# The expert table's layout and its fetch, and new setup lists, in a one-core transformer block

## The reference, cut to what matters

```python
# x: (32, 512, 256), float32; D = 256, F = 512, E = 8 experts
h = layernorm(x) * (1 + ca) + sa                      # per row, modulation from c @ wmod
S = scan(s = a*s + (1-a)*h)                            # over the 512 tokens
x = x + ga * (S @ W.T + b + conv5(h) + conv_b)
h = layernorm(x) * (1 + cb) + sb
sel = argmax(gelu(h[:, -1] @ Wp1 + bp1) @ Wp2 + bp2)   # one expert of 8 for each row
y = gelu(h @ W1[sel] + b1[sel]) @ W2[sel] + b2[sel]
x = x + gb * (h + 0.3 * (y @ Wo + bo))
```

## Time and profile before

| | us |
|---|---|
| median of 3 runs (lowest, highest) | 654.22 (653.48, 655.22) |
| the profiled execution, its own time | 653.61 |
| its span, first to last instruction | 651.8 |
| TensorE, busy in the span | 633.2 |
| VectorE / ScalarE / GpSimd, busy | 568.0 / 551.1 / 439.4 |

### The profile page before, as it was taken

How to read it: one execution, slowest core, us unless ns; L and a number is a source line. 1 busy time by engine, 2 the same in 40 slices (tenths; PEclk the granted TensorE clock), 3 DMA queues, 4 the chain that set the end, 5 groups by cost and what they waited for, 6 DMA issues and landing times.

```text
span 651.8 us, 11098 instructions
## 1 busy us (share of the span) xinstructions
PE 633.2 (97%) x3405; PEld 521.6 (80%) x3405; DVE 568.0 (87%) x895; ACT 551.1 (85%) x976; POOL 439.4 (67%) x536
## 2 busy tenths in 40 slices
PE   7898899999999999999999999999999999999996
PEld 7686687888788888888888888888888888888865
DVE  1686889999899999999999999999999999998712
ACT  3797788889888988889988988888988898887763
POOL 2774676776677676776667667677666767677543
PEclk9999999999999999999999999999999999999999
DMA  9999635455445455455544545554544455543442
GB/s 297 329 358 298 212 135 194 139 186 167 166 158 191 162 193 194 148 185 175 172 165 163 189 167 194 176 185 158 194 146 170 171 175 183 193 162 111 172 165 104
DMA packets 55454, 120.58 MB, mean 185 GB/s; under 512 B 5643, under 2 KB 43364, under 8 KB 46180
## 3 DMA queue, kind: packets, MB, share of 16 engines
q1 hardware_dynamic: 51844, 115.65, 51.9%
q10 hardware_dynamic: 3552, 4.23, 2.0%
HBM read 61.12 MB, written 25.19 MB: 132 GB/s over the span
## 4 chain that ended last, share of the span: by engine, by line
PE 84%; DMA 7%; POOL 3%; DVE 2%; ACT 2%; issue 1%; SPq 1%; DVEq 0%; ACTq 0%; POOLq 0%
PE U L1062 10%; PE U L1063 9%; PE U L1064 9%; PE Q L1077 9%; PE Q L1078 8%; PE Q L1082 8%; PE TR L1102 8%; PE Q L1094 4%; PE Y L1046 4%; PE Y L1043 4%; PE Y L1042 4%; PE TR L1094 4%; DMA up_w<-up_table 3%; DMA xr<-in_L_attn_x_dram 2%; DMA xr<-in_L_ffn_W_dram 2%; PE U L1117 2%
## 5 line engine op out<-in xcount | busy, mean ns | idle before, releaser
L452 POOL TENSOR_TENSOR g_lo<-g,g_hi 128x512 fp32r<-128x512 f32 x128 | 173.8, 1358 | 90.0 <-ACT g_hi L613 85.0
L839 DVE SCALAR_TENSOR_TENSOR Y<-h,taps,Y 128x512 f32<-128x512 f32 x320 | 224.7, 750 | 2.9 <-PE Y L1046 0.7
L1062 PE MATMUL U<-hid_hi,up_w 128*128 128x512 f32 x256 | 107.4, 419 | 2.2 <-DMA up_w<-up_table 2.2
L1077 PE MATMUL Q<-g_hi,down_w 128*128 128x512 f32 x256 | 106.2, 415 | 0.0
L565 ACT ACTIVATE S<-xr,nmr,rstd 128x256 f32<-128x256 f32 x128 | 66.6, 592 | 42.6 <-POOL S_lo L460 40.1
L1063 PE MATMUL U<-hid_hi,up_w 128*128 128x512 f32 x256 | 101.4, 396 | 0.0
L1078 PE MATMUL Q<-g_hi,down_w 128*128 128x512 f32 x256 | 101.1, 395 | 0.0
L1064 PE MATMUL U<-hid_lo,up_w 128*128 128x512 f32 x256 | 100.8, 394 | 0.0
L787 DVE BATCH_NORM_STATS2 st<-xr 128x6 f32<-128x512 f32 x128 | 88.4, 712 | 9.4 <-DMA xr<-in_L_attn_x_dram 4.9
L606 ACT ACTIVATE g<-U,up_w 128x512 f32<-128x512 f32 x128 | 88.1, 688 | 8.6 <-PE U L1064 7.0
L435 POOL TENSOR_SCALAR rstd<-st 128x4 f32<-128x4 f32 x64 | 26.5, 413 | 87.2 <-DVE st L787 84.5
(11 more groups left out here) (115 smaller groups left out, 1293.7 us busy)
## 6 DMA issues: line engine op xcount, KB each, us to landing
up_w<-up_table SPq DMA_DIRECT2D x32, 1027.0 KB, 6.2
down_w<-down_tab SPq DMA_DIRECT2D x32, 1024.0 KB, 4.7
xr<-in_L_attn_x_dram SPq DMA_DIRECT2D x32, 512.0 KB, 3.6
out_dram<-xr SPq DMA_DIRECT2D x64, 256.0 KB, 2.3
xr<-in_L_ffn_W_dram ACTq DMA_DIRECT2D x5, 512.0 KB, 11.6
xr<-in_L_ffn_W_dram SPq DMA_DIRECT2D x4, 512.0 KB, 9.4
up_table<-g_lo SPq DMA_DIRECT2D x2, 1024.0 KB, 10.2
up_table<-down_w SPq DMA_DIRECT2D x2, 1024.0 KB, 9.3
```

The lines of the kernel that those rows point to most:

```text
L452: nc.gpsimd.tensor_tensor(g_lo[:, f], g[:, f % 2], g_hi[:, f].bitcast(f32), ALU.subtract).then_inc(g_lo_ready, 1)
L839: ins = nc.vector.scalar_tensor_tensor(out=Y[c][:, :], in0=h[:, c, k:k + T], scalar=taps[:, c, k:k + 1], in1=Y[c][:, :], op0=ALU.mult, op1 ...
L1062: mm(U[f % 2][:, :], up_w[:, par, UP + w:UP + w + P], hid_hi[:, par, c], start=(c == 0), stop=False)
L1077: mm(Q[c][:, :], down_w[:, par, 1, w:w + P], g_hi[:, f], start=(f == 0), stop=False)
```

## The change

**Layout.** The table's row now begins with b1 and the bias, and the split W1 comes after them by quarters f of its 512 columns: for each f, the rounded numbers of both channel chunks, then the remainders of both. `by_f` is that view. `w1_hi` and `w1_lo` write in this order, and `up(i, f)` reads quarter f. All tiles of weights that TensorE reads are still 128 by 128 and contiguous in a partition.

**Fetch.** The fetch is two transfers: the first brings b1, the bias and the quarters 0 and 1 (4120 bytes in a partition), the second the quarters 2 and 3 (4096 bytes). `up(i, 0)` and `gate_beta` wait for the first, `up(i, 2)` for the second, the copy to `down_w` for the second. `fetch` is cut into `fetch_up` and `fetch_down`, and `load_x(i + 5)` now stands between them, behind the two transfers, where it was in front.

**Setup lists.** The orders of the setup on SP, GpSimd, ScalarE, VectorE and TensorE are new. The instructions are the same but for the two forms above; the slots' lists other than SP's are not touched.

```diff
 DOWN = FC * D
-U_B1 = 2 * UP
+U_B1 = 0
 U_BETA = U_B1 + FC
-UPW = U_BETA + DC
+U_W = U_BETA + DC
+UPW = U_W + 2 * UP
+U_HALF = U_W + UP
...
     split_room += [down_w[:, 0].rearrange("p k n -> p (k n)"), down_w[:, 1].rearrange("p k n -> p (k n)"),
-                   up_w[:, 0, 0:2 * UP], up_w[:, 1, 0:2 * UP], split_room[2]]
+                   up_w[:, 0, U_W:UPW], up_w[:, 1, U_W:UPW], split_room[2]]
+    def by_f(room):
+        return room.rearrange("p (f k c n) -> p f k c n", k=2, c=DC, n=P)
...
     up_loaded = [sem("up_loaded0"), sem("up_loaded1")]
+    up_half_loaded = [sem("up_half_loaded0"), sem("up_half_loaded1")]
     down_loaded = [sem("down_loaded0"), sem("down_loaded1")]
...
             sp.wait_ge(s_w1_lo, e + 1)
-            sp.dma_start(up_table[e, :, 0:2 * UP], split_room[e].bitcast(f32)).then_inc(s_split_out[e // 2], 16)
+            sp.dma_start(up_table[e, :, U_W:UPW], split_room[e].bitcast(f32)).then_inc(s_split_out[e // 2], 16)
...
             sp.wait_ge(s_beta3, DC)
-            sp.dma_start(up_table.rearrange("e p n -> p e n")[:, :, U_BETA:UPW], beta3[:, :, :]).then_inc(s_params, 16)
+            sp.dma_start(up_table.rearrange("e p n -> p e n")[:, :, U_BETA:U_W], beta3[:, :, :]).then_inc(s_params, 16)
         def prologue():
+            load_x(0)
             vectors()
+            load_w1(0)
             load_w2(0)
+            load_wo()
             load_w()
-            load_x(0)
-            load_wo()
+            load_w2(1)
+            load_w1(1)
             load_taps()
-            load_router()
-            load_w1(0)
-            load_w1(1)
-            load_w2(1)
             load_x(1)
...
             load_w2(2)
-            b1_out()
             load_w1(2)
+            load_w1(3)
...
             split_out(0)
-            load_w1(3)
...
             load_w1(4)
+            beta_out()
+            b1_out()
             split_out(1)
+            split_out(2)
             load_w1(5)
             load_w1(6)
-            split_out(2)
             split_out(3)
-            split_out(4)
-            beta_out()
+            load_router()
...
             load_w1(7)
+            split_out(4)
             split_out(5)
-            split_out(6)
...
             load_x(3)
+            split_out(6)
             split_out(7)
-        def fetch(r):
-            par, half = r % 2, r // 2
+        def fetch_up(r):
+            par = r % 2
             if r == 0:
...
             e = sp.value_load(sel8[0:1, par, 0:1], min_val=0, max_val=E - 1)
-            sp.dma_start(up_w[:, par].bitcast(f32), up_table[bass.ds(e, 1)].rearrange("o p n -> p (o n)")).then_inc(up_loaded[par], 16)
+            table = up_table[bass.ds(e, 1)].rearrange("o p n -> p (o n)")
+            sp.dma_start(up_w[:, par, 0:U_HALF].bitcast(f32), table[:, 0:U_HALF]).then_inc(up_half_loaded[par], 16)
+            sp.dma_start(up_w[:, par, U_HALF:UPW].bitcast(f32), table[:, U_HALF:UPW]).then_inc(up_loaded[par], 16)
+            return e
+        def fetch_down(r, e):
+            par = r % 2
             if r == 0:
...
                     sp.dma_start(tok(out[i - 1])[:, ts], xr[:, (i - 1) % NX, ts]).then_inc(stored[(i - 1) % 2], 16)
+            if row(i + 1):
+                e = fetch_up(i + 1)
             if row(i + 5):
...
             if row(i + 1):
-                fetch(i + 1)
+                fetch_down(i + 1, e)
         for q in stored:
...
             pool.wait_ge(s_w1_hi, e + 1)
-            room = split_room[e]
-            nc.gpsimd.tensor_tensor(room[:, UP:2 * UP], w1_nat(e).rearrange("p c f -> p (c f)"),
-                                    room[:, 0:UP].bitcast(f32), ALU.subtract).then_inc(s_w1_lo, 1)
+            room = by_f(split_room[e])
+            nc.gpsimd.tensor_tensor(room[:, :, 1], w1_nat(e).rearrange("p c (f n) -> p f c n", n=P),
+                                    room[:, :, 0].bitcast(f32), ALU.subtract).then_inc(s_w1_lo, 1)
...
             wait(pool, hid_gated_ready, DC * r)
-            pool.wait_ge(up_loaded[r % 2], 16 * (r // 2 + 1))
-            nc.gpsimd.tensor_tensor(gbeta[:, :], up_w[:, r % 2, U_BETA:UPW].bitcast(f32), mods[:, GB:GB + DC, r],
+            pool.wait_ge(up_half_loaded[r % 2], 16 * (r // 2 + 1))
+            nc.gpsimd.tensor_tensor(gbeta[:, :], up_w[:, r % 2, U_BETA:U_W].bitcast(f32), mods[:, GB:GB + DC, r],
                                     ALU.mult).then_inc(gbeta_ready, 1)
...
             norm1(1)
-            s_low0(0)
             w1_lo(1)
             w1_lo(2)
+            s_low0(0)
+            w1_lo(3)
             gates()
-            w1_lo(3)
             norm1(2)
+            s_low0(1)
             w1_lo(4)
-            s_low0(1)
             norm2(0)
...
             w1_lo(7)
+            hid_low(0)
             s_low0(2)
             norm1(3)
-            hid_low(0)
...
                 act.wait_ge(s_split_out[1], 32)
-            nc.scalar.copy(split_room[e][:, 0:UP], w1_nat(e).rearrange("p c f -> p (c f)")).then_inc(s_w1_hi, 1)
+            nc.scalar.copy(by_f(split_room[e])[:, :, 0], w1_nat(e).rearrange("p c (f n) -> p f c n", n=P)).then_inc(s_w1_hi, 1)
...
         def prologue():
-            w2T_copy(0)
             xn1_of(0)
             w1_hi(0)
+            w2T_copy(0)
             h_of(0)
-            down_high(0, 0)
-            down_high(0, 1)
-            mix_high()
             w2T_copy(1)
...
             s_high(0, 1)
+            down_high(0, 0)
             w1_hi(1)
+            w2T_copy(2)
+            w1_hi(2)
+            down_high(0, 1)
             down_high(1, 0)
-            w1_hi(2)
+            mix_high()
             xn1_of(1)
-            w2T_copy(2)
             w1_hi(3)
             down_high(1, 1)
-            w1_hi(4)
             w2T_copy(3)
             down_high(2, 0)
+            down_high(2, 1)
             h_of(1)
-            down_high(2, 1)
+            w1_hi(4)
+            down_high(3, 0)
             gate1(0)
             s_high(1, 0)
+            down_high(3, 1)
             w2T_copy(4)
-            down_high(3, 0)
+            s_high(1, 1)
             w1_hi(5)
             w1_hi(6)
-            down_high(3, 1)
-            s_high(1, 1)
             w2T_copy(5)
+            xn2_of(0)
+            w1_hi(7)
+            down_high(4, 0)
+            down_high(4, 1)
+            w2T_copy(6)
             xn1_of(2)
-            down_high(4, 0)
-            xn2_of(0)
-            down_high(4, 1)
             hid_of(0)
-            w2T_copy(6)
-            w1_hi(7)
             down_high(5, 0)
-            gate1(1)
+            down_high(5, 1)
             h_of(2)
-            down_high(5, 1)
             w2T_copy(7)
             down_high(6, 0)
-            down_high(6, 1)
+            hid_high(0)
             nav_of(0)
             s_high(2, 0)
+            gate1(1)
+            down_high(6, 1)
+            down_high(7, 0)
             s_high(2, 1)
-            hid_high(0)
-            down_high(7, 0)
             down_high(7, 1)
...
             mods_setup()
+            scan(0, 0)
+            scan(0, 1)
+            stats1(1)
+            s_low1(0)
             down_low(0, 0)
-            stats1(1)
-            scan(0, 0)
+            betas()
+            down_low(0, 1)
+            down_low(1, 0)
             mix_low()
-            down_low(0, 1)
-            scan(0, 1)
-            betas()
-            s_low1(0)
             dve.wait_ge(s_taps, 16)
             conv(0, 0, 6)
-            down_low(1, 0)
-            conv(0, 6, 9)
             down_low(1, 1)
+            down_low(2, 0)
+            conv(0, 6, 10)
+            scan(1, 0)
             stats1(2)
-            conv(0, 9, 10)
-            down_low(2, 0)
-            scan(1, 0)
             down_low(2, 1)
             scan(1, 1)
+            down_low(3, 0)
+            down_low(3, 1)
             residual1(0, 0)
-            down_low(3, 0)
+            residual1(0, 1)
             s_low1(1)
-            residual1(0, 1)
-            down_low(3, 1)
             conv(1, 0, 6)
...
             down_low(5, 0)
+            stats1(3)
             down_low(5, 1)
             scan(2, 0)
+            down_low(6, 0)
             scan(2, 1)
-            stats1(3)
-            down_low(6, 0)
+            router(0)
             down_low(6, 1)
-            router(0)
+            down_low(7, 0)
             residual1(1, 0)
+            s_low1(2)
             residual1(1, 1)
-            s_low1(2)
-            down_low(7, 0)
             down_low(7, 1)
...
             if f == 0:
-                pe.wait_ge(up_loaded[par], 16 * (i // 2 + 1))
+                pe.wait_ge(up_half_loaded[par], 16 * (i // 2 + 1))
                 pe.wait_ge(hid_lo_ready, DC * (i + 1))
...
             wait(pe, gelu_out, n - 1)
+            if f == 2:
+                pe.wait_ge(up_loaded[par], 16 * (i // 2 + 1))
+            w = by_f(up_w[:, par, U_W:UPW])[:, f]
             for c in parts:
-                w = c * F + f * P
```

(34 more changed lines are left out.)

## The result

| | median us (range, runs) | profiled execution: span, mean clock |
|---|---|---|
| before | 654.13 (652.08 to 655.85, 20) | 651.8, 0.998 |
| changed | 656.09 (653.04 to 662.16, 20) | 651.3, 0.995 |

The ratio is 1.0041 [1.0024, 1.0057]: slower, where 652.1 was forecast. The profiled execution of the changed kernel took 653.04 us, the fastest of its 20; the kernel before spread over 3.8 us, the changed kernel over 9.1. So this one trace shows the change at its best, and the experiments have to tell the rest.

A forecast was written before the change was run, and what follows sets the result against it. TensorE was taken to bound the slots, any further gain coming from the setup. Setup -0.8, table waits -1.5 and late x +0.2 took 653.61 to 651.5, plus 0.6 for the median: 652.1 us, range 650.5 to 654.

The forecast's parts named there:

- The setup, -0.8: Setup: `up(0, 0)` starts 2.7 us earlier, of which slot 0 lets 0.8 us through.
- The waits and the late x, -1.5 and +0.2: Slots: two TensorE waits for the table vanish, saving 1.5 us; a few late x loads cost 0.2 us.
- The step from the profiled execution to the median, +0.6: Whole kernel: the median of the runs lies 0.6 us above the profiled execution, raising 651.5 to 652.1.
- Item 4: Setup, VectorE: `down_low(2, 1)` ends at 41.0, `comb(3, 1)` idles 2.9 us for it, `mix(1)` ends at 49.5.
- the lists lose: Rival, setup: late `mix(0)` and `down_low` are not recovered, `up(0, 0)` near 77, total 655 to 657; chance 0.15.
- Item 1: Setup start: x(0) is issued first, making the modulation vectors some 0.5 us later, not on the path yet.
- Items 5 to 7: Late setup: W1(7) lands at about 50.5, TensorE needs 18.95 us plus two short waits, `up(0, 0)` starts at 72.6.
- What slot 0 keeps: Slot 0: `router_nav(1)` is tied to `hid_of(1)`, so only 0.8 of the setup's 2.7 us gets through.
- The layout, "nothing" to +0.7: Rounding on ScalarE and remainder on GpSimd: no change taken, 0.7 us more at the high end.
- The fetch in two, -1.5: Slots: the first half lands 3.3 to 5 us after issue, removing TensorE's table waits; 1.5 us saved at most.
- x behind the fetch, +0.2: Slots: x lands 7.8 us after the fetch's issue, needed at 8.6; a few long ones cost 0.2 us.
- The rival's +4 to +6 us: Rival, slots: x lands late behind the fetch, costing 4 to 6 us, total 656 to 658; chance 0.10.

The follow-up runs named there:

- e4: The changed kernel measured again with no edit, its profiled execution taking 656.53 us: median 657.99 us, ratio 1.0070 to the kernel before.
- e13: The whole changed kernel with ten unused floats in front of b1 in each table row: 653.27 us, ratio 0.9984 to the kernel before.
- e15: e13 with 20 unread transposes of the identity between `comb(3, 0)` and `comb(3, 1)`: 652.08 us, ratio 0.9965 to the kernel before.
- e10: The changed kernel with 20 unread transposes of the identity between `comb(3, 0)` and `comb(3, 1)`: 657.44 us, ratio 1.0047 to the kernel before.
- e12: The kernel before with ten unused floats at the end of each table row (8256 bytes apart in DRAM): 651.82 us, ratio 0.9960.
- e2: The kernel before with the five new setup lists, layout and fetch left as before: 656.43 us, ratio 1.0036 to the kernel before.
- e17: The kernel before with two unused floats at the end of each table row (8224 bytes apart in DRAM): 651.19 us, ratio 0.9946.
- e6: e1 with the whole table fetched in one transfer behind x, as before, so only the layout is new: ratio 1.0033 to the kernel before.
- e9: e1 with ten unused floats in front of b1 (table rows of 8256 bytes): 651.53 us, ratio 0.9961 to the kernel before.
- e5: The kernel before measured again with no edit, for a second trace: 654.02 us, ratio 0.9997.
- e7: e1 with x in front of the fetch in halves, as before, instead of behind it: ratio 1.0019 to the kernel before.
- e1: The changed kernel with the five setup lists of before, keeping the new layout and fetch: 656.41 us, ratio 1.0035 to the kernel before.
- e16: The kernel before with b1 and the bias moved in front of the weights in a row, no quarters, no halves: ratio 1.0009.
- e3: The changed kernel with `down_low(2, 1)` moved before `scan(1, 0)` and `stats1(2)` on VectorE: 658.94 us, ratio 1.0062 to the kernel before.
- e14: e9 with DRAM table rows as in the changed kernel (8216 bytes apart), padding kept only in the SBUF tile: 656.55 us, ratio 1.0034.
- e8: e6 with the split W1 at the row's start and b1 and the bias behind it: ratio 1.0009 to the kernel before.

## Why the prediction was wrong

The median was forecast 2 us below before and came 2 us above, 4.0 us from the forecast. The sum had four terms. The setup, -0.8: nav came 0.2 us later than before instead, 1.0 off. The waits and the late x, -1.5 and +0.2: the rest became 0.7 shorter, 0.6 off. The step from the profiled execution to the median, +0.6, taken over from the kernel before: the changed kernel's is 3.05, 2.45 off, and this is the largest miss. So the walk was near for the fastest execution (651.5 forecast, 653.04 measured), and the step that failed most is that one execution's landings and pace were taken to hold for all. What stands behind the 3.05, e4 shows: 1.6 us by the half pace at the start, 1.7 by the later W2(6), and nearly the same rest (570.8). How often each comes among the 20 runs is not known. The queue has a large part: with rows that begin well, the changed kernel's median is 653.27 (e13), what its fastest execution takes without the padding.

1. *Item 4, the gap before `comb(3, 1)`.* Forecast 41.0 and 2.9 us of idle, measured 41.29 and 2.84. Then the forecast let the comb run at full speed. At 1.2 GHz it took 1.5 us more; `mix(1)` ended near 51.1 instead of 49.5, and `comb(4, 0)` began at 51.12, the point from which the forecast let the lists lose. The medians of e15 and e13 put this at 1.2 us of the end, e4 and e10 at 1.4 us of `comb(4, 0)`. It is the step that failed for the lists: a gap was priced by its length alone. On padded rows and with the gap filled the whole change is level with the padding alone (e15 0.9965, e12 0.9960).
2. *Item 1.* With x(0) first in the queue the first matmul started at 3.5 to 3.7 instead of 2.5 to 2.7 us, in all seven traces with the new lists, and the transpose of the vectors at 7.7 to 8.2 instead of 6.2 to 6.8. The forecast had 0.5 us and "not on the path". Where the half pace was added to it, `comb(3, 0)` began at 38.2 (e4, e10, e15) instead of 36.5 to 36.9 (the four others); how much of the late start alone reaches the end was not measured.
3. *Items 5 to 7* were right in the profiled execution once shifted: W1(7) landed at 50.3 (50.5 forecast), though `w1_hi(7)` ran at 53.1 (50.8), behind `xn2_of(0)`; fetch at 69.95 (68.5), `up(0, 0)` 74.18 (72.6). "18.95 us of work and two short waits", 20.4 together, took 20.1. In e2, e4 and e10, W2(6) at 57.5 to 58 (54 in the profile) undid it: `up(0, 0)` at 79.5, 77.5, 78.6. The forecast took landings of before over to lists that lean more on the queue, without asking how much they vary.
4. *What slot 0 keeps.* Right in kind: nav waited for `hid_of(1)`. The forecast kept 0.8 of 2.7 us; of the 1.1 us that the setup gained nothing was left.
5. *The layout, "nothing" to +0.7.* `w1_lo` took 2.36 us as before, so the term was right for the two engines that it looked at. The writes of the table were in no term. Where their rows begin decides when W2(6) lands, in the kernel before too (52.6 and 50.3, against 46.8 and 46.5 in e12 and e17); e6's +0.33% comes on top, and what in the layout causes it stays open. On padded rows the same layout costs nothing (e9, e12).
6. *The fetch in two, -1.5.* The waits for `up_w` went, as predicted (3.9 us to landing; the estimate of 3.2 us by the Trainium skill, "DMA: Bandwidth & Descriptors", section "Anatomy of one DMA", was too short; that section is on transfers issued from GpSimd, and these are issued from SP). But the rest became 0.7 us shorter, not 1.3, and in e5, the kernel before once more, it was 570.9, 0.3 from the changed kernel's 570.6. In e9, `up(0, 0)` came 1.3 us earlier than in e12 and the rest was 1.3 longer, TensorE waiting for `g_lo` (0.6) and `down_w` (0.2) instead. Worth about nothing.
7. *x behind the fetch, +0.2*: 1.7 us of VectorE waits, no more, and e7 beside e1, where only the place of x differs, 1.0019 and 1.0035, intervals that overlap. The rival's +4 to +6 us is out; up to about 1 us is not. The nearest rival, "the lists lose" (655 to 657; its own price, +2 to +3.5 less 1.5, gives 654.7 to 656.2), had the time and the point, 51 us, but not the mechanism, and its `up(0, 0)` near 77 was at 74.18 in the profile. Luck had a part in its time: e1, with none of the new lists, lost as much.

The fastest kernel of all is e17: before, with two unused floats in a table row and nothing of the change.

## What to carry to other kernels

Before reordering around a full transfer queue, see what it moves per microsecond and whether the rows that it writes in DRAM begin on 32 bytes: here two padding floats gave 0.5%, and a long hand-made order gave nothing. Price a TensorE gap of 2 to 3 us with what followed such gaps here, some 1.5 us at 1.2 GHz, and look for one that the change opens even where the idle time as such is bought back. When setup and queue are tight, one trace says little about a kernel's median: trace a second execution near the median, as e4, and take the spread of the runs as part of the result.

## What the runs showed of the hardware that was not expected

- The granted clock fell to 0.50 in or behind single TensorE gaps of 1.71 (e7), 2.09 (e6), 2.21 (e16), 2.47 and 2.85 (e2), 2.69 (e10), 2.83 (e4), 2.84 (after, e13), 2.96 (e3) and 3.02 us (e1), and behind 1.08 and 0.90 us close together (e3); it stayed at 1.00 behind 1.64 (e14), 1.66 (e4) and 1.88 us (e8). So between 1.7 and 1.9 us the length of the gap did not decide by itself. The clock was back at 1.00 within 3 to 6 us of the gap's end in each.
- Filler transposes kept it at 1.00 and made `comb(4, 0)` earlier by 1.4 us (e10 beside e4) and the median lower by 1.2 us (e15 beside e13, intervals that just overlap).
- DMA writes of 1 MB into DRAM rows 8216 bytes apart landed in 8.2 to 10.2 us (medians), into rows of 8224 in 4.0 to 7.8 (e17), in the same queue. The start in SBUF made no difference (e14 1.0034, e1 1.0035), nor did the start in DRAM for reads (6.2 us before, 6.4 in e17).
- The same kernel ran its first matmuls at full pace from 8.3 us in one execution and from 12.5 in another (after, e4), with the granted clock given as 1.00 in both.
